# A two-attention transformer block on one core: batch loops written out, score products over all 128 rows, and the mask product in bf16

## The chip, the cores and the metric

The kernel runs on 1 core of one Trainium2 chip. The metric is the device time of one execution in microseconds (us). TensorE's clock has two levels here, 1.2 and 2.4 GHz; a granted clock of 1.00 is the higher one.

## What is computed

Input x is 8 x 512 x 512 in float32. The reference, cut to its steps:

```
attention(x):                        # per batch: seq 512, 16 heads of 32
    Q, K, V = x W^T + (x A^T) B^T    # each with a low-rank term (rank 16) whose matrices an adapter index picks
    Q, K = rope(Q), rope(K)
    P = softmax(where(causal, Q K^T / sqrt(32), -inf))
    return out W_o^T + low-rank term, with out = P V
x1 = layernorm(x + attention(x))
second(x1):                          # hidden 512, feed-forward 2048
    a   = causal attention of rmsnorm(x1) with its own weights, then W_o
    mod = 0.1 tanh(a A)
    h   = rmsnorm(x1)
    return x1 + (silu(h W_in^T + (mod * (h A)) B) * (h W_up^T)) W_down^T
result = layernorm(x1 + second(x1))
```

All products are made in about float32 precision: an operand is split into a high part in float32r (hi) and the rest (lo), and a product is hi*hi + hi*lo + lo*hi.

## The kernel before

The program has three stages one behind the other: `attention_layer` (names `a_`), `gate_layer` (names `b_`, the output projection, first layernorm, second attention down to the modulation) and `mlp_layer` (names `c_`). Each engine runs its own instruction list, and semaphores order them.

Both attention stages have one skeleton. A batch is four groups of four heads. A group is twelve slots, one for each unit; a head has three units, with score widths 512, 384 and 256 + 128 columns (`KEY_MAJOR`, line 36). In slot k of a group the engines do, in this order written out by hand:

- TensorE: `score_t_unit` (line 259), the transposed scores key x q of unit k, and on top of them the causal mask as one more product, eye x colmask, 128 columns wide (line 271). In slots 1 to 7 it also makes `score_unit` (line 174), the plain scores of the next group, which serve only for the row maxima. Then come shares of projections and, two units behind, the product of probabilities and values (`pv_unit`, line 293). In slot 8 it turns the negated row maxima of the next group into rows (`shift_turn`, line 217).
- ScalarE: two exponentials of the scores (lines 281 and 282), copies out of PSUM, and in slot 9 the copy and the transfer of the turned maxima (`shift_copy`, `shift_send`).
- VectorE: the lo part of the probabilities (line 289), and in slots 1 to 7 the masked row maxima (line 199).
- SP: the transfers. `stack_send` (line 242) builds, for two heads at a time and two groups ahead, the operands of the score products.

The stacks are what the change is about. For each head q_stack has q hi in rows 0 to 31, q hi again in 32 to 63 and q lo in 64 to 95; k_stack has key hi, key lo, key hi. One product over these rows makes the three split products at once. Rows 96 to 127 are set once by GpSimd: 0 in q_stack, 1 in k_stack. Rows 112 and 113 of q_stack then take the two parts of the negated row maximum (`shift_send`, line 234), which the ones of k_stack add to the transposed scores. So the plain scores are made over 112 rows (they must not see the maximum), and the transposed ones over 114. A pair of heads is complete when its semaphore `stacked` has risen by 96: six transfers of 16. TensorE waits for that before unit 0 and unit 6 (line 179). ScalarE waits for it before it overwrites the split q or key (lines 745 and 1479).

`batches` (line 65) makes the loop over batches. Batch 0 is written out; then a loop with a branch back runs the same body (batches 1 to 6 in the first stage, 1 to 5 in the second, where `ahead` is 2), and the last one or two are written out again. Inside the loop the batch number is a register, so `apart` (line 54) lets the engine compute the awaited count and then wait for it. With a plain number it is one wait on a constant.

## Time and profile before

| | us |
|---|---|
| median of 3 runs | 2967.54 (2967.21 to 2971.47) |
| the profiled execution | 2964.34 |
| its span, first to last instruction | 2962.5 |
| TensorE busy | 2721.6 (92%) |
| VectorE, ScalarE, GpSimd busy | 1586.3, 1342.3, 645.6 |
| mean granted TensorE clock | 0.955 |

In the rows, PE is TensorE's products, PEld its weight loads, DVE VectorE, ACT ScalarE, POOL GpSimd and SPq the transfers that SP issues. L271 is line 271 of the kernel. A shape like 114x512 is partitions x elements. Products are pipelined, so their durations overlap; the distance between starts tells what one takes from the stream. What stands in brackets behind a row is how long the engine was idle before it and what ended that. "issue" is idle time in which nothing was awaited that the profile shows.

### The profile page before, as it was taken

Reading aid. Unit: us, or ns where it says so; the run is one execution under the profiler, and the core shown is the slowest. Engines: PE = TensorE matmul, PEld = TensorE weight load, DVE = VectorE, ACT = ScalarE, POOL = GpSimd, SP = SyncE. Lnnn points to the kernel's source line nnn. Section 1 sums busy time; section 2 is a strip of 40 time slices with the busy share of each in tenths; the row PEclk is TensorE's granted clock in tenths of the full one; section 3 lists DMA queues with packets and bytes.
Section 4 is the critical chain, followed back from the end, with each engine's and each line's share of the span. In section 5 each row is a group of like instructions: output and inputs, shape, how many; then the busy total and the mean of one; then the engine's idle time right before and its main releaser. Section 6 shows DMA issues by size and latency. Waiting matters only on the chain. (4 is left out here: it accounts for less than half of the span.)

```text
span 2962.5 us, 46172 instructions
## 1 busy us (share of the span) xinstructions
PE 2721.6 (92%) x13840; PEld 2174.2 (73%) x13840; DVE 1586.3 (54%) x4308; ACT 1342.3 (45%) x2755; POOL 645.6 (22%) x528
## 2 busy tenths in 40 slices
PE   5999999999758999999999994999999999999998
PEld 4778777787636777777777762888888888888886
DVE  3777777777634776777777773422222333333333
ACT  2777677766633666656656664311111231111111
POOL 5455555555321122122122112000000000000000
PEclk8999999999867999999999996999999999999999
DMA  5455555555624544544545543311111121111100
GB/s 140 100 135 132 134 116 133 129 129 116 151 83 118 124 96 115 130 90 112 133 91 118 117 89 97 117 58 49 44 44 44 66 87 46 58 44 45 44 29 29
DMA packets 173888, 276.05 MB, mean 93 GB/s; under 512 B 29204, under 2 KB 53524, under 8 KB 173076
## 3 DMA queue, kind: packets, MB, share of 16 engines
q1 hardware_dynamic: 170772, 260.58, 36.3%
q0 software_dynamic: 2304, 12.58, 1.2%
q10 hardware_dynamic: 640, 1.05, 0.1%
q8 instruction: 52, 0.85, 0.1%
q14 instruction: 120, 0.98, 0.1%
HBM read 97.04 MB, written 42.99 MB: 47 GB/s over the span
## 5 line engine op out<-in xcount | busy, mean ns | idle before, releaser
L2224 DVE TENSOR_TENSOR c_product<-c_up_ps,c_gate 128x512 f32<-128x512 f32 x128 | 88.6, 692 | 653.3 <-PE c_up_ps L2290 653.3
L2278 PE MATMUL c_gate_ps<-c_h_split,c_w_split 128*128 128x512 f32 x1536 | 380.8, 397 | 23.6 <-DVE c_w_split L2176 23.6
L2262 PE MATMUL c_down_ps<-c_w_split,c_product_split 128*128 128x512 f32 x1536 | 379.3, 396 | 0.0
L2290 PE MATMUL c_up_ps<-c_h_split,c_w_split 128*128 128x512 f32 x1536 | 378.2, 395 | 0.0
L2278 PEld LDWEIGHTS c_gate_ps<-c_h_split,c_w_split 128*128 128x128 f32 x1536 | 290.0, 189 | 95.3 <-issue 25.3
L2290 PEld LDWEIGHTS c_up_ps<-c_h_split,c_w_split 128*128 128x128 f32 x1536 | 288.4, 188 | 70.0
L2262 PEld LDWEIGHTS c_down_ps<-c_w_split,c_product_split 128*128 128x128 f32 x1536 | 288.9, 188 | 68.6
L281 ACT ACTIVATE b_prob_hi<-b_scores_t_ps 128x384 fp32r<-128x384 f32 (+1 forms) x384 | 201.1, 524 | 266.0 <-PE b_scores_t_ps L271 230.1
L289 DVE TENSOR_TENSOR b_prob_lo<-b_scores_t_ps,b_prob_hi 128x384 fp32r<-128x384 f32 (+1 forms) x384 | 225.8, 593 | 148.9 <-ACT b_scores_t_ps L282 137.3
L289 DVE TENSOR_TENSOR a_prob_lo<-a_scores_t_ps,a_prob_hi 128x384 fp32r<-128x384 f32 (+1 forms) x384 | 226.2, 593 | 145.3 <-ACT a_scores_t_ps L282 140.3
L2148 ACT ACTIVATE c_gate<-c_gate_ps 128x512 f32<-128x512 f32 x128 | 76.4, 597 | 492.4 <-PE c_gate_ps L2285 492.4
L281 ACT ACTIVATE a_prob_hi<-a_scores_t_ps 128x384 fp32r<-128x384 f32 (+1 forms) x384 | 201.3, 524 | 161.7 <-PE a_scores_t_ps L271 136.6
L199 DVE CUSTOM_DVE_ANT_0 b_junk<-b_scores_ps,rowmask 128x512 bf16<-128x512 f32 (+3 forms) x512 | 226.7, 482 | 71.4 <-PE b_scores_ps L185 47.4
L199 DVE CUSTOM_DVE_ANT_0 a_junk<-a_scores_ps,rowmask 128x512 bf16<-128x512 f32 (+3 forms) x512 | 227.0, 484 | 59.4 <-PE a_scores_ps L185 35.8
L2151 ACT ACTIVATE c_product_split<-c_product 128x512 fp32r<-128x512 f32 x128 | 81.0, 633 | 390.5 <-DVE c_product L2224 390.5
L977 PE MATMUL a_lin_ps<-x_split,w_split 128*128 128x512 f32 x768 | 225.7, 412 | 0.4 <-DVE w_split L831 0.4
L268 PE MATMUL b_scores_t_ps<-b_q_stack,b_k_stack 114*128 114x512 f32 (+3 forms) x512 | 159.7, 354 | 51.0 <-DVE b_prob_lo L289 50.0
L1850 PE MATMUL b_lin_ps<-b_h_split,w_split 128*128 128x512 f32 x768 | 203.1, 404 | 1.2 <-ACT b_h_split L1473 1.2
L282 ACT ACTIVATE a_scores_t_ps<-a_scores_t_ps 128x384 f32<-128x384 f32 (+1 forms) x384 | 201.4, 524 | 0.0
L282 ACT ACTIVATE b_scores_t_ps<-b_scores_t_ps 128x384 f32<-128x384 f32 (+1 forms) x384 | 200.7, 523 | 0.0
L268 PE MATMUL a_scores_t_ps<-a_q_stack,a_k_stack 114*128 114x512 f32 (+3 forms) x512 | 154.5, 343 | 42.7 <-DVE a_prob_lo L289 42.6
L268 PEld LDWEIGHTS b_scores_t_ps<-b_q_stack,b_k_stack 114*128 114x128 f32 x512 | 95.9, 200 | 104.4 <-DVE b_prob_lo L289 74.5
(205 smaller groups left out, 4969.8 us busy)
## 6 DMA issues: line engine op xcount, KB each, us to landing
a_q_stack<-a_q_split SPq DMA_DIRECT2D x192, 128.0 KB, 3.2
a_k_stack<-a_k_split SPq DMA_DIRECT2D x192, 128.0 KB, 3.5
b_q_stack<-b_q_split SPq DMA_DIRECT2D x192, 128.0 KB, 3.3
b_k_stack<-b_k_split SPq DMA_DIRECT2D x192, 128.0 KB, 3.6
c_h_stage<-h_t SPq DMA_DIRECT2D x16, 1024.0 KB, 6.2
c_res<-x SPq DMA_DIRECT2D x16, 1024.0 KB, 5.5
c_w_stage<-in_mlp_w POOLq DMA_DIRECT2D x16, 768.0 KB, 4.5
stage<-in_x_t SPq DMA_DIRECT2D x8, 1024.0 KB, 6.4
```

What stands on the lines that cost most here:

```text
L199: last = dve.tensor_tensor_reduce(at.junk[:, k % 2, col:col + width], at.scores_ps[:, k % 2, col:col + width], rowmask[:, SEQ - width:SEQ] ...
L268: pe.matmul(at.scores_t_ps[:, k % 2, col:col + width], key[0:STACK_ROWS, h, kt * P:kt * P + P], q[0:STACK_ROWS, h, kt * P:SEQ], start=(i = ...
L281: act.activation(at.prob_hi[:, k % at.ring, 0:w], at.scores_t_ps[:, k % 2, 0:w], ACT.Exp, scale=SCALE)
L282: act.activation(at.scores_t_ps[:, k % 2, 0:w], at.scores_t_ps[:, k % 2, 0:w], ACT.Exp, scale=SCALE).then_inc(at.exp_done, 1)
L289: dve.tensor_tensor(at.prob_lo[:, k % at.ring, 0:w], at.scores_t_ps[:, k % 2, 0:w], at.prob_hi[:, k % at.ring, 0:w], ALU.subtract).then_in ...
L977: mm = pe.matmul(lin_ps[:, bank, :], w_split[i][:, w, c, g * P:g * P + P], x_split[:, a, c, :], start=(x == 0), stop=False)
L1850: mm = pe.matmul(lin_ps[:, i, :], qk_split[i][:, w, c, g * P:g * P + P], h_split[:, a, c, :], start=(x == 0), stop=(x == 3 * KC - 1))
L2151: act.activation(product_split[:, bank, 0, :], product[:, bank, :], ACT.Copy).then_inc(product_hi, 1)
L2224: dve.tensor_tensor(product[:, bank, :], up_ps[:, bank, :], gate[:, bank, :], ALU.mult).then_inc(product_done, 1)
L2262: mm = pe.matmul(down_ps[:, t, :], product_split[:, kt % 2, a, t * P:t * P + P], w_split[:, w, kt, 2 * KC * P:], start=(kt == 0 and i == 0 ...
L2278: pe.matmul(gate_ps[:, bank, :], w_split[:, w, ft, c * 2 * P:c * 2 * P + P], h_split[run.pair][:, a, c, :], start=(c == 0 and w == 0 and a ...
L2290: mm = pe.matmul(up_ps[:, bank, :], w_split[:, w, ft, c * 2 * P + P:(c + 1) * 2 * P], h_split[run.pair][:, a, c, :], start=(c == 0 and w = ...
```

## The change

- The loop over the batches becomes straight code in both attention stages, and every wait on a computed count becomes a wait on a constant.
- Both kinds of score products take all 128 rows of the stacks. So that the plain scores don't see the row maxima of two groups before, `stack_send` clears rows 112 and 113 of q_stack with one more transfer per pair of heads, from rows 116 and 117, which are always zero. A pair is then complete at 7 x 16 = 112.
- The mask product takes bf16 copies of eye and colmask. eye stays in float32r too, for the turning of the maxima.
- At the start SP waits until GpSimd has also set the q stacks, and TensorE for three constants instead of two.

The diff, without the hunks that only pass `eye_bf` on and with `gate_layer`'s twins of the changed waits left out:

```diff
@@ -38,7 +38,8 @@
 WIDTH = (512, 384, 384)
 
 
-SPLIT_ROWS, SHIFT_ROW, STACK_ROWS = 112, 112, 114
+STACKED = 7 * 16
+SHIFT_ROW, SHIFT_END, SPARE_ROW = 112, 114, 116
 
 
 COS, SIN, EYE, ROWMASK, COLMASK, COUNT = 0, 512, 1024, 1152, 1664, 1792
@@ -64,11 +65,7 @@
 
 def batches(eng, body, ahead=1):
 
-
-    body(0)
-    with eng.Fori(1, BATCH - ahead) as b:
-        body(b)
-    for b in range(BATCH - ahead, BATCH):
+    for b in range(BATCH):
         body(b)
 
 
@@ -97,7 +94,8 @@
         self.x_split = sb("x_split", [P, 2, KC, SEQ], F32R)
         self.rowmask = sb("rowmask", [P, SEQ])
         self.eye = sb("eye", [P, P], F32R)
-        self.colmask = sb("colmask", [P, P], F32R)
+        self.eye_bf = sb("eye_bf", [P, P], BF16)
+        self.colmask = sb("colmask", [P, P], BF16)
         self.lnw = sb("lnw", [P, 2, KC])
 
 
@@ -176,14 +174,14 @@
     h, j = divmod(k, 3)
     n = number(b, g)
     if k % (UNITS // 2) == 0:
-        pe.wait_ge(at.stacked[h // 2], n * 96 + 96)
+        pe.wait_ge(at.stacked[h // 2], n * STACKED + STACKED)
     if k == 0:
         at_least(pe, at.shift_copied, n)
     at_least(pe, at.score_read, n * UNITS + k - 1)
     q, key = at.q_stack[g % 2], at.k_stack[g % 2]
     for i, (qt, col, width) in enumerate(QUERY_MAJOR[j]):
-        mm = pe.matmul(at.scores_ps[:, k % 2, col:col + width], q[0:SPLIT_ROWS, h, qt * P:qt * P + P],
-                       key[0:SPLIT_ROWS, h, 0:(qt + 1) * P], start=(i == 0), stop=True, skip_group_check=True)
+        mm = pe.matmul(at.scores_ps[:, k % 2, col:col + width], q[:, h, qt * P:qt * P + P],
+                       key[:, h, 0:(qt + 1) * P], start=(i == 0), stop=True, skip_group_check=True)
     mm.then_inc(at.score_ready, 1)
 
 
@@ -235,7 +233,7 @@
 
     n = number(b, g)
     act.wait_ge(at.shift_copied, n + 1)
-    act.dma_start(at.q_stack[g % 2][SHIFT_ROW:STACK_ROWS, :, :].bitcast(F32),
+    act.dma_start(at.q_stack[g % 2][SHIFT_ROW:SHIFT_END, :, :].bitcast(F32),
                   at.shift_row[0:2 * GH, :].bitcast(F32)).then_inc(at.shifted, 16)
 
 
@@ -250,13 +248,15 @@
     for r, part in enumerate((0, 0, 1)):
         sp.dma_start(q[32 * r:32 * r + 32, heads, :].bitcast(F32),
                      at.q_split[rows, part, :].bitcast(F32)).then_inc(at.stacked[pair], 16)
+    sp.dma_start(q[SHIFT_ROW:SHIFT_END, heads, :].bitcast(F32),
+                 q[SPARE_ROW:SPARE_ROW + SHIFT_END - SHIFT_ROW, heads, :].bitcast(F32)).then_inc(at.stacked[pair], 16)
     apart(sp, at.ones_set, at.k_ready, n + 1)
     for r, part in enumerate((0, 1, 0)):
         sp.dma_start(key[32 * r:32 * r + 32, heads, :].bitcast(F32),
                      at.k_split[rows, part, :].bitcast(F32)).then_inc(at.stacked[pair], 16)
 
 
-def score_t_unit(pe, at, eye, colmask, b, g, k):
+def score_t_unit(pe, at, eye_bf, colmask, b, g, k):
 
     h, j = divmod(k, 3)
     n = number(b, g)
@@ -265,10 +265,10 @@
     at_least(pe, at.lo_done, n * UNITS + k - 1)
     q, key = at.q_stack[g % 2], at.k_stack[g % 2]
     for i, (kt, col, width) in enumerate(KEY_MAJOR[j]):
-        pe.matmul(at.scores_t_ps[:, k % 2, col:col + width], key[0:STACK_ROWS, h, kt * P:kt * P + P],
-                  q[0:STACK_ROWS, h, kt * P:SEQ], start=(i == 0), stop=False, skip_group_check=True)
+        pe.matmul(at.scores_t_ps[:, k % 2, col:col + width], key[:, h, kt * P:kt * P + P],
+                  q[:, h, kt * P:SEQ], start=(i == 0), stop=False, skip_group_check=True)
     for kt, col, width in KEY_MAJOR[j]:
-        mm = pe.matmul(at.scores_t_ps[:, k % 2, col:col + P], eye[:, :], colmask[:, :],
+        mm = pe.matmul(at.scores_t_ps[:, k % 2, col:col + P], eye_bf[:, :], colmask[:, :],
                        start=False, stop=True, skip_group_check=True)
     mm.then_inc(at.score_t_ready, 1)
 
@@ -596,7 +596,7 @@
             for n, w in ((1, wk_t), (2, wv_t)):
                 for c in range(KC):
                     sp.dma_start(w_stage[n][c], w[:, c, :]).then_inc(w_in[n], 16)
-            sp.wait_ge(rows_zeroed, 2)
+            sp.wait_ge(rows_zeroed, 4)
             send_b(0)
             send_low(0)
             for pair in range(2):
@@ -742,7 +742,7 @@
                 n = number(b, g)
                 act.wait_ge(roped[i], n * 3 + 3)
                 for pair in range(2):
-                    at_least(act, at.stacked[pair], n * 96)
+                    at_least(act, at.stacked[pair], n * STACKED)
                 split = at.k_split if i else at.q_split
                 act.activation(split[:, 0, :], rope_out[i][:, :], ACT.Copy).then_inc(rope_hi[i], 1)
 
@@ -823,6 +823,7 @@
             dve.wait_ge(ids_step, 2 + ADAPTERS)
             dve.tensor_scalar(ids[:, :], count[:, :], 0.0, None, ALU.max).then_inc(ids_step, 1)
             dve.tensor_copy(eye[:, :], square[:, 0, :]).then_inc(const_ready, 1)
+            dve.tensor_copy(eye_bf[:, :], square[:, 0, :]).then_inc(const_ready, 1)
             dve.tensor_copy(colmask[:, :], square[:, 1, :]).then_inc(const_ready, 1)
 
             def weights(n):
@@ -943,7 +944,7 @@
 
         @block.tensor
         def _(pe):
-            pe.wait_ge(const_ready, 2)
+            pe.wait_ge(const_ready, 3)
             pe.wait_ge(rows_zeroed, 4)
             pe.wait_ge(at.ones_set, 3)
 
@@ -1334,7 +1335,7 @@
             sp.dma_start(stage[:, :, :], wo).then_inc(stage_in, 16)
             sp.dma_start(a_full[:, :, :], low_a).then_inc(const_in, 16)
             sp.dma_start(sel[:, :], selector).then_inc(const_in, 16)
-            sp.wait_ge(rows_zeroed, zeroed_before + 2)
+            sp.wait_ge(rows_zeroed, zeroed_before + 4)
             send_b(0)
             send_low(0)
             sp.wait_ge(wo_a_made, 1)
```

## Rows read from the trace of the kernel before

**Rows 1.** Busy time by stretch: us, busy per engine (instructions), clock, DMA share, GB/s.

```profile
0.00:870.00 870.00, 752.29 (x4448) 624.22 (x4448) 584.20 (x1743) 561.34 (x1175) 447.75 (x351) 0.94 0.54 127
870.00:1842.00 972.00, 862.97 (x4656) 658.55 (x4656) 662.25 (x1916) 560.17 (x1191) 190.47 (x164) 0.92 0.48 106
1842.00:2962.00 1120.00, 1106.39 (x4736) 891.41 (x4736) 339.81 (x650) 220.77 (x390) 7.39 (x14) 0.99 0.17 56
```

**Rows 2.** Timeline of TensorE, second stage, line 222: start us, us, instruction.

```profile
1268.56 0.40 PE L222 MATMUL b_scores_ps<-eye,b_shift 128*8 128x128 f32 x4
...
1296.88 0.40 PE L222 MATMUL b_scores_ps<-eye,b_shift 128*8 128x128 f32 x4
...
1607.52 0.40 PE L222 MATMUL b_scores_ps<-eye,b_shift 128*8 128x128 f32 x4
...
1631.67 0.40 PE L222 MATMUL b_scores_ps<-eye,b_shift 128*8 128x128 f32 x4
```

**Rows 3.** Timeline of VectorE at a branch back of the second stage.

```profile
1277.06 0.56 DVE L289 TENSOR_TENSOR b_prob_lo<-b_scores_t_ps,b_prob_hi 128x384 fp32r<-128x384 f32 x1 [2.72 <-issue]
```

**Rows 4.** Busy time and clock right behind that branch, columns as in rows 1.

```profile
1278.00:1284.00 6.00, 6.00 (x23) 4.84 (x23) 4.97 (x16) 4.51 (x11) 0.00 (x0) 0.50 0.93 163
```

**Rows 5.** Timeline of TensorE, first stage, line 222.

```profile
161.26 0.41 PE L222 MATMUL a_scores_ps<-eye,a_shift 128*8 128x128 f32 x4
...
185.95 0.40 PE L222 MATMUL a_scores_ps<-eye,a_shift 128*8 128x128 f32 x4
...
545.21 0.41 PE L222 MATMUL a_scores_ps<-eye,a_shift 128*8 128x128 f32 x4
...
570.99 0.40 PE L222 MATMUL a_scores_ps<-eye,a_shift 128*8 128x128 f32 x4
```

**Rows 6.** Who waited for whom: us in total, times, longest.

```profile
DVE b_junk L199 <- issue: 22.2, 33, 1.3
...
ACT b_prob_hi L281 <- PE b_scores_t_ps L271: 230.1, 216, 3.0
...
ACT b_q_split L1481 <- DMA b_k_stack<-b_k_split: 15.8, 8, 10.2
```

**Rows 7.** Timeline of TensorE, first stage, one single-piece and one two-piece unit.

```profile
406.79 0.34 PE L268 MATMUL a_scores_t_ps<-a_q_stack,a_k_stack 114*128 114x384 f32 x1
406.97 0.22 PE L271 MATMUL a_scores_t_ps<-colmask,eye 128*128 128x128 f32 x1
407.03 1.16 PE L977 MATMUL a_lin_ps<-x_split,w_split 128*128 128x512 f32 x4
...
408.38 0.39 PE L268 MATMUL a_scores_t_ps<-a_q_stack,a_k_stack 114*128 114x256 f32 x2
408.61 0.39 PE L271 MATMUL a_scores_t_ps<-colmask,eye 128*128 128x128 f32 x2
408.83 0.45 PE L977 MATMUL a_lin_ps<-x_split,w_split 128*128 128x512 f32 x1
```

**Rows 8.** Instructions on the tile eye: count, ns min/median/max, first and last start.

```profile
L271 PEld LDWEIGHTS b_scores_t_ps<-colmask,eye x512: 186/191/339, 946.2 to 1803.0; 128*128 128x128 f32 x171
...
L1833 PEld LDWEIGHTS b_lin_ps<-eye,stage x128: 137/144/232, 898.0 to 1678.5; 128*128 128x128 f32 x128
```

**Rows 9.** Timeline of SP's queue, first stage: one pair's q transfers.

```profile
406.22 1.88 SPq L251 DMA_DIRECT2D a_q_stack<-a_q_split  x3
```

**Rows 10.** Timeline of TensorE, first stage: the wait for the key rows.

```profile
413.18 0.49 PE L185 MATMUL a_scores_ps<-a_k_stack,a_q_stack 112*128 112x512 f32 x1 [0.91 <-DMA a_k_stack<-a_k_split]
```

**Rows 11.** Timeline of TensorE: its first product.

```profile
14.03 1.49 PE L961 MATMUL a_lin_ps<-x_split,a_a_split 128*48 128x512 f32 x3 [14.03 <-DVE a_b_split L855]
```

**Rows 12.** Line 623: count, ns min/median/max, first and last start.

```profile
L623 POOL MEMSET a_q_stack<- x2: 1799/1801/1803, 3.5 to 5.3; 32x2048 f32 x2
```

**Rows 13.** Timeline of TensorE, second stage: fp32 transposes between fp32r products.

```profile
1117.07 0.71 PE L1833 MATMUL b_lin_ps<-eye,stage 128*128 128x128 f32 x4
1117.53 0.42 PE L268 MATMUL b_scores_t_ps<-b_q_stack,b_k_stack 114*128 114x384 f32 x1
```

More of the change, by code:

```diff
@@ L428, in attention_layer @@
         ids, w_split, x_stage, x_split = both.ids, both.w_split, both.stage, both.x_split
-        rowmask, eye, colmask = both.rowmask, both.eye, both.colmask
+        rowmask, eye, eye_bf, colmask = both.rowmask, both.eye, both.eye_bf, both.colmask
         a_stage = sb("a_stage", [P, KC, 3 * RANK])
@@ L1020, in step @@
                 for slot in range(UNITS):
-                    score_t_unit(pe, at, eye, colmask, b, g, slot)
+                    score_t_unit(pe, at, eye_bf, colmask, b, g, slot)
                     if not (last and g == GROUPS - 1):
@@ L1146, in gate_layer @@
         values = lin_ps[:, :, :].rearrange("p i (t h d) -> p (i t) h d", t=2, d=RANK)
-        ids, lnw, rowmask, eye, colmask = both.ids, both.lnw, both.rowmask, both.eye, both.colmask
+        ids, lnw, rowmask, eye, eye_bf, colmask = both.ids, both.lnw, both.rowmask, both.eye, both.eye_bf, both.colmask
         wo_split, *qk_split = both.w_split
@@ L1478, in projected @@
                 for pair in range(2):
-                    at_least(act, at.stacked[pair], n * 96)
+                    at_least(act, at.stacked[pair], n * STACKED)
                 split = at.k_split if i else at.q_split
@@ L1889, in step @@
                 for slot in range(UNITS):
-                    score_t_unit(pe, at, eye, colmask, b, g, slot)
+                    score_t_unit(pe, at, eye_bf, colmask, b, g, slot)
                     if slot == 2 and g == 0 and not last:
```

## The prediction, made before the change was run

> **What bounds the kernel now.** I read the stretches first. The span falls into three stages [rows 1]. Up to 870 us runs the first attention, up to 1842 us the second, and the rest is the feed-forward stage, which none of the edited functions reaches: its 1120 us stay. In the two attention stages TensorE is the busiest engine (752 of 870 us and 863 of 972 us), and VectorE and ScalarE have about a third of the time free. So TensorE's stream sets the pace there, broken by places where it waits. Three things are to be priced: what the loops' branches cost, what the mask product costs in that stream, and what the new transfers delay. The sum is made against the profiled execution: 2964.3 us, of which the span is 2962.5. The median of the runs shown is 2967.5, so 3.2 us are added at the end. A change within 0.2% (5.9 us) is about what a measurement of this kernel can't tell from none.
>
> **The loops written out.** A mark that comes once per group is the turning of the shifts (line 222, always in slot 8). The interval from the mark in a batch's last group to the next mark, in the first group of the next batch, holds the batch boundary. In the second stage the loop covers batches 1 to 5, so four boundaries take the branch back. I take one of the middle two as typical: 28.32 us [rows 2]. The boundary from batch 5 to 6 leaves the loop without a branch back and does the same work: 24.15 us [rows 2]. That is 4.2 us for each of four: **16.7 us**. The waits say where it comes from. At that branch VectorE stands 2.72 us on "issue", that is with nothing it waits for in the profile [rows 3], and TensorE, which needs its product, stands too. After that gap TensorE's granted clock is at the lower of its two levels, 1.2 GHz, for 6 us [rows 4]. Part of this is absorbed, which is why I take the interval and not the sum of the pieces. In the first stage the loop covers batches 1 to 6, five branches back. The interval of the middle length is 25.78 us, and the entry from batch 0, without a branch, 24.69 us [rows 5]: 1.09 us, times five, is **5.5 us**. Together 22.2 us.
>
> Inside the loops the waits on a computed count cost VectorE another 22.2 us of "issue" in the second stage, about as much in the first [rows 6]. Written out they become waits on constants. I cost this at nothing: TensorE's own stream hides it. Its bounds are 0 and twice the row, 44 us; I take 0, the end that the busy shares are nearest to, as VectorE is free a third of the time.
>
> **The mask product.** Each of 768 units adds the causal mask with line 271: 1024 products, two in every third unit. In the stream, a product over 384 columns is followed after 0.18 us by the mask product, and that after 0.06 us by the next start [rows 7]. So fp32r already streams 128 columns in 0.06 us, and bf16 can't gain there. In a unit with two pieces the starts stand otherwise: two products take 0.23 us and two masks 0.22 us, so the starts come every 0.11 us [rows 7]. The moving columns of a mask need only 0.06 us of that; what is left is the weights' load, an instruction of its own that can't run further ahead than the product before. If bf16 makes this load shorter than 0.06 us, each of the two masks starts 0.05 us sooner: 0.10 us per such unit. The product behind the last mask loads fp32r weights and still comes 0.11 us after it, so single masks bring nothing. 256 units times 0.10 us are 25.6 us, the upper end. The lower end is nothing, if the load takes as long as now; a loss is a rival below. How much of it reaches the end? In the second stage ScalarE's exponentials waited for the mask product in 216 of 384 units [rows 6]; there the gain is passed on in full, elsewhere only through TensorE's stream. Between half and all I take 0.7: 25.6 x 0.7 = **17.9 us**. I take the fast load because the nearest row for another kind of operand, the plain fp32 transposes, shows that the load depends on the kind: 144 ns against 191 ns for this one [rows 8]. No row has a bf16 load.
>
> The Trainium skill has two sentences on this that disagree for this kernel, both in "TensorE: Matmul & The Clock Gate". Its section "LDWEIGHTS (loading the stationary operand)" counts columns alone, which is 107 ns for 128 columns of any type; by it the mask gains nothing and rival (1) comes true. Its section "Weight-path perf modes — Fast Weight Load (FWL) and DoubleRow" says that the load goes about twice as fast when there are 128 weights and the type is not FP32; by it a load would take an estimated 53 ns and the whole term is there. No run here shows a bf16 load yet.
>
> **128 rows.** The score products now use all 128 rows instead of 112 and 114. Rows seem to have no price: two-piece units load 114 rows and 128 rows at the same 0.11 us [rows 7]. Cost: none. Bounds: nothing below, and above half a nanosecond for each of 14 to 16 rows in 2048 products, 16 us, were rows paid like columns (0.18 us for 384); I take none, as the loads show.
>
> **The clearing transfers.** They are two more on SP's queue in each of 64 groups, between the three for q and the three for key, each 0.6 us of issue, as three take 1.88 us [rows 9]. Everything behind them on that queue moves: the key rows, the store of the group before, the next gather. Mostly this is hidden, because the stacks are sent a group before they are used; without that cover 128 x 0.6 = 77 us. The cover is gone once per batch of the first stage: behind the low-rank sends the key rows come late, and TensorE waits 0.91 us for them [rows 10]. 0.6 us more in each of seven batches: 4.2 us. A longer wait also makes a low clock behind it likelier; two more drops of some 3 us at half speed [rows 4] cost 3 us. In the second stage ScalarE waits for the stacks before it splits the next q, 8 times [rows 6]. Its wait grows by the second pair's 0.6 us; half of 8 x 0.6 reaches the end, with the first pair's in part behind SP's own waits: 2 us. Together **9.2 us** lost. Bounds: 2, since SP's register work for waits goes away, and 15, if the clock drops in every batch. The wait for four zeroed tiles instead of two and the second constant copy lie at the start, where TensorE's first product waits 14.03 us for VectorE's split of the adapters [rows 11]; without that cover they cost the two memsets, 3.6 us [rows 12].
>
> **Sum.** 2964.3 - 22.2 - 17.9 + 9.2 = 2933.4 us, plus 3.2: **2937 us**.
>
> **The rivals.**
> (1) *The bf16 load is no faster.* For it: no row shows one, and loads of 114 and 128 rows take the same time, so columns seem to rule. Against it: rows 8. The mask term is gone: 2964.3 - 22.2 + 9.2 + 3.2 = **2954 us**.
> (2) *The change of kind stalls the array.* Where a bf16 product stands between fp32r ones, TensorE would have to run empty before it and behind it. The price is the part of a 128-column product that now overlaps the next: 0.22 us long, 0.06 us to the next start, so 0.16 us, twice in 768 units: 246 us, and the time would be **3200 us**. It decides from 13 us / 768 = 17 ns a unit. Against it: four fp32 transposes pass between fp32r products, and the fp32r product starts 0.46 us after their first, 0.115 us each, without a gap [rows 13].
> (3) *Straight code stalls too.* The instructions of written-out batches come from memory just the same, and stands like the 2.72 us could come at other places as often as now. Then the 22.2 us are not gained: 2964.3 - 17.9 + 9.2 + 3.2 = **2959 us**, or 2977 us with a slow load. Against it: batch 6 of the second stage is written out today, and its boundary has none of it [rows 2].
>
> **How the numbers follow.** Forecast 0.58, with 2922 to 2945 as its own range; (1) 0.30, (3) 0.07, (2) 0.05. The whole range takes in the forecast with the whole mask gain and a small loss (2964.3 - 22.2 - 25.6 + 4 + 3.2 = 2924), a few us below it for the register waits that I cost at nothing, and rival (1) with the transfers' upper bound (2954 + 6 = 2960): 2918 to 2960. Faster by more than 0.2% (below 2961.6): both main cases and the smaller part of (3), 0.90. Within 0.2%: 0.03. Slower: (2) and the rest of (3), 0.07.
>
> **What would show it.** The intervals of line 222 across every batch boundary should be near 24.2 us in the second and 24.7 us in the first stage, and VectorE's "issue" stands of 2.7 us gone. The mask's load should be well under 190 ns, and two-piece units should take 0.35 us to the next start instead of 0.45. The wait for the key rows in the first stage should be longer by up to 0.6 us. The forecast is wrong if mask loads stay at 190 ns, if gaps stand around line 271, if "issue" shows up elsewhere, or if the key rows' wait is followed by low clock in most batches.

## The result, and the profile after

The changed kernel took 2932.7 us (median; 2929.3 to 2934.3), the kernel before 2967.4 us beside it. The ratio is 0.9879, with a 95% interval of 0.9862 to 0.9896: 1.2% faster, and 34.6 us by the medians. The forecast was 2937 us, with 2918 to 2960 as its range.

| | before | after |
|---|---|---|
| median, us | 2967.4 | 2932.7 |
| the profiled execution / its span | 2964.3 / 2962.5 | 2934.3 / 2932.4 |
| TensorE products busy / weight loads busy | 2721.6 / 2174.2 | 2685.4 / 2053.0 |
| VectorE, ScalarE busy | 1586.3, 1342.3 | 1584.6, 1335.6 |
| instructions in the trace | 46172 | 41577 |
| mean granted TensorE clock | 0.955 | 0.969 |

Here are the profile after's stretches, with the columns of [rows 1]. The first three are the stages, and the fourth is where the branch's low clock stood before [rows 4].

```profile
0.00:860.00 860.00, 747.85 (x4448) 572.05 (x4448) 584.90 (x1744) 557.63 (x1173) 441.30 (x348) 0.95 0.53 127
860.00:1812.00 952.00, 830.83 (x4656) 590.79 (x4656) 660.49 (x1917) 557.66 (x1194) 196.38 (x167) 0.96 0.47 111
1812.00:2932.00 1120.00, 1106.77 (x4736) 890.16 (x4736) 339.22 (x649) 220.34 (x389) 7.39 (x14) 0.99 0.17 56
...
1276.00:1284.00 8.00, 8.00 (x49) 5.95 (x47) 5.90 (x16) 5.91 (x13) 2.60 (x2) 1.00 0.93 228
```

The feed-forward stage is what it was, 1120 us. The second attention stage gives 20 us (972 to 952) and the first 10 (870 to 860). Counted more closely, from each attention's first mark (the turning of the shifts, line 222 before) to its last, the second goes from 847.6 to 825.3 us, the first from 759.6 to 755.9, and the way from one to the other from 114.3 to 110.3. So almost all of the gain lies in the second stage and ahead of it, and the first stage gives 4 us.

The changed kernel's timeline, all engines. Line 220 is now the mark (222 before), 268 the transposed scores, 271 the mask (PEld its loads), 978 the first projections; SPq lines 249, 251 and 255 are q's transfers, the clearing and key's transfers.

```profile
406.61 0.34 PE L268 MATMUL a_scores_t_ps<-a_q_stack,a_k_stack 128*128 128x384 f32 x1
406.79 0.23 PE L271 MATMUL a_scores_t_ps<-colmask,eye_bf 128*128 128x128 bf16 x1
406.83 1.18 PE L978 MATMUL a_lin_ps<-x_split,w_split 128*128 128x512 f32 x4
...
408.20 0.39 PE L268 MATMUL a_scores_t_ps<-a_q_stack,a_k_stack 128*128 128x256 f32 x2
408.43 0.28 PE L271 MATMUL a_scores_t_ps<-colmask,eye_bf 128*128 128x128 bf16 x2
408.43 0.12 PEld L271 LDWEIGHTS a_scores_t_ps<-colmask,eye_bf 128*128 128x128 bf16 x2
408.52 1.18 PE L978 MATMUL a_lin_ps<-x_split,w_split 128*128 128x512 f32 x4
409.54 0.39 PE L985 MATMUL a_lin_ps<-a_low_stack,a_b_stack 128*128 128x512 f32 x1
...
405.87 1.88 SPq L249 DMA_DIRECT2D a_q_stack<-a_q_split  x3
407.79 0.66 SPq L251 DMA_DIRECT2D a_q_stack<-a_q_stack  x1
408.49 1.85 SPq L255 DMA_DIRECT2D a_k_stack<-a_k_split  x3
...
371.27 0.59 ACT L315 ACTIVATE a_pv_raw<-a_pv_ps 65x512 f32<-65x512 f32 x1 [2.78 <-DMA a_sums<-a_pv_raw]
...
544.21 0.40 PE L220 MATMUL a_scores_ps<-eye,a_shift 128*8 128x128 f32 x4
...
570.58 0.40 PE L220 MATMUL a_scores_ps<-eye,a_shift 128*8 128x128 f32 x4
...
1254.80 0.40 PE L220 MATMUL b_scores_ps<-eye,b_shift 128*8 128x128 f32 x4
...
1277.89 0.55 DVE L289 TENSOR_TENSOR b_prob_lo<-b_scores_t_ps,b_prob_hi 128x384 fp32r<-128x384 f32 x1
...
1278.60 0.41 PE L220 MATMUL b_scores_ps<-eye,b_shift 128*8 128x128 f32 x4
...
1577.95 0.40 PE L220 MATMUL b_scores_ps<-eye,b_shift 128*8 128x128 f32 x4
...
1601.76 0.41 PE L220 MATMUL b_scores_ps<-eye,b_shift 128*8 128x128 f32 x4
```

Four things are to be read there. *The boundaries*: from 1254.80 to 1278.60 is 23.80 us, where the branch had made it 28.32 [rows 2]; the last, from 1577.95 to 1601.76, is 23.81 (24.15 before). VectorE's L289 at 1277.89 has no bracket: the stand of 2.72 us [rows 3] is gone, and the granted clock behind it is full instead of half. *The first stage's boundaries* moved little: 544.21 to 570.58 is 26.37 us, 25.78 before [rows 5]; the five at issue have a mean of 25.5, before 25.7. *The mask*: in the two-piece unit the next product comes 0.09 us after the two masks began, where it was 0.22 [rows 7]. That next product itself then takes a little longer: from its line's first start to the next line's is 1.02 us (408.52 to 409.54) instead of 0.98. The net in this unit is 0.09 us. *ScalarE at 371.27* stands 2.78 us for the transfers of the group's sums. Before, it reached this place later and stood 0.45 us. The two rows of the kernel before on which the last two readings rest (its timeline):

```profile
409.81 0.39 PE L984 MATMUL a_lin_ps<-a_low_stack,a_b_stack 128*128 128x512 f32 x1
...
371.20 0.59 ACT L315 ACTIVATE a_pv_raw<-a_pv_ps 65x512 f32<-65x512 f32 x1 [0.45 <-DMA a_sums<-a_pv_raw]
```

The changed kernel's instructions on the identity in bf16 (count, ns min/median/max, first and last start):

```profile
L271 PEld LDWEIGHTS a_scores_t_ps<-colmask,eye_bf x512: 95/96/149, 74.0 to 840.5; 128*128 128x128 bf16 x171
...
L271 PEld LDWEIGHTS b_scores_t_ps<-colmask,eye_bf x512: 95/96/147, 939.8 to 1772.0; 128*128 128x128 bf16 x171
```

The bf16 load is 96 ns, half of 191 [rows 8]. The changed kernel's waits (us in total, times, longest):

```profile
ACT b_prob_hi L281 <- PE b_scores_t_ps L271: 205.1, 181, 3.0
...
PEld a_scores_t_ps L271 <- issue: 42.3, 195, 0.5
...
ACT a_pv_raw L315 <- DMA a_sums<-a_pv_raw: 27.8, 21, 3.2
...
ACT b_q_split L1482 <- DMA b_k_stack<-b_k_split: 20.8, 8, 10.4
...
ACT b_pv_raw L315 <- DMA b_sums<-b_pv_raw: 17.6, 8, 4.0
...
PE a_scores_ps L183 <- DMA a_k_stack<-a_k_split: 15.5, 11, 7.6
```

VectorE's wait on "issue" in the score maxima (22.2 us in 33 pieces, [rows 6]) is gone. The 42.3 us of "issue" ahead of the mask's loads are new, but they are idle time of the loads alone: TensorE's products have no stand on "issue" in either attention. In the second stage ScalarE waits less for the mask product: 181 times for 205 us, before 216 times for 230. It waits more for the sums' transfers: 27.8 and 17.6 us, where the kernel before had these two rows (its waits):

```profile
ACT a_pv_raw L315 <- DMA a_sums<-a_pv_raw: 10.1, 10, 1.9
...
ACT b_pv_raw L315 <- DMA b_sums<-b_pv_raw: 7.8, 4, 3.0
```

And the wait for the key rows, which the prediction expected to grow, is 15.5 us in total in the first stage, as before (15.9), though in 11 pieces instead of 9.

### The profile page after: what moved, and what is told of

It reads as the page before. It is cut to its first block and busy times, and to the rows that moved or that the text cites. A ratio compares the mean times of both kernels' runs of the same rounds, so it can differ in the third digit from the quotient of the medians.

```text
span 2932.4 us, 41577 instructions
## 1 busy us (share of the span) xinstructions
PE 2685.4 (92%) x13840; PEld 2053.0 (70%) x13840; DVE 1584.6 (54%) x4309; ACT 1335.6 (46%) x2755; POOL 645.1 (22%) x528
## 5 line engine op out<-in xcount | busy, mean ns | idle before, releaser
L289 DVE TENSOR_TENSOR a_prob_lo<-a_scores_t_ps,a_prob_hi 128x384 fp32r<-128x384 f32 (+1 forms) x384 | 226.3, 594 | 151.6 <-ACT a_scores_t_ps L282 149.4
L289 DVE TENSOR_TENSOR b_prob_lo<-b_scores_t_ps,b_prob_hi 128x384 fp32r<-128x384 f32 (+1 forms) x384 | 226.1, 594 | 135.8 <-ACT b_scores_t_ps L282 134.3
L268 PE MATMUL b_scores_t_ps<-b_q_stack,b_k_stack 128*128 128x512 f32 (+3 forms) x512 | 153.3, 340 | 50.0 <-DVE b_prob_lo L289 45.6
L268 PE MATMUL a_scores_t_ps<-a_q_stack,a_k_stack 128*128 128x512 f32 (+3 forms) x512 | 152.8, 340 | 42.3 <-DVE a_prob_lo L289 42.1
L183 PE MATMUL a_scores_ps<-a_k_stack,a_q_stack 128*128 128x512 f32 (+3 forms) x512 | 147.7, 371 | 20.2 <-DMA a_k_stack<-a_k_split 15.5
```

What stands on the lines that cost most here:

```text
L183: mm = pe.matmul(at.scores_ps[:, k % 2, col:col + width], q[:, h, qt * P:qt * P + P], key[:, h, 0:(qt + 1) * P], start=(i == 0), stop=True ...
L268: pe.matmul(at.scores_t_ps[:, k % 2, col:col + width], key[:, h, kt * P:kt * P + P], q[:, h, kt * P:SEQ], start=(i == 0), stop=False, skip ...
L289: dve.tensor_tensor(at.prob_lo[:, k % at.ring, 0:w], at.scores_t_ps[:, k % 2, 0:w], at.prob_hi[:, k % at.ring, 0:w], ALU.subtract).then_in ...
```

## The experiments

Twelve runs, in three groups; "before" was run beside each group (medians 2966.3, 2965.7 and 2964.3 us), and the ratios are to it. They are built from three parts: the loops, the bf16 mask, and the 128 rows with their clearing. None changes what is computed. The last column is the mean granted clock over all executions of a kernel; that of the kernel before was 0.959 beside each group.

| kernel | loops | mask | clearing | rows | median, us | ratio to before | clock |
|---|---|---|---|---|---|---|---|
| e1_unroll | written out | fp32r | none | 112, 114 | 2939.2 | 0.9911 [0.9895, 0.9927] | 0.963 |
| e2_mask | as before | bf16 | none | 112, 114 | 2956.0 | 0.9965 [0.9951, 0.9979] | 0.959 |
| e3_rows | as before | fp32r | yes | 128, 128 | 2969.1 | 1.0012 [1.0003, 1.0021] | 0.964 |
| e4_unroll_mask | written out | bf16 | none | 112, 114 | 2932.8 | 0.9876 [0.9857, 0.9895] | 0.963 |
| e5_no_bf16 | written out | fp32r | yes | 128, 128 | 2936.9 | 0.9903 [0.9883, 0.9922] | 0.967 |
| e6_two_per_turn | two batches a turn | fp32r | none | 112, 114 | 2963.1 | 0.9987 [0.9976, 0.9998] | 0.962 |
| e7_three_clears | written out | bf16 | three a pair | 128, 128 | 3027.6 | 1.0201 [1.0183, 1.0219] | 0.958 |
| e8_one_mask | written out | bf16, one product | none | 112, 114 | 2925.8 | 0.9861 [0.9843, 0.9878] | 0.963 |
| e9_clears_only | written out | bf16 | yes | 112, 114 | 2938.4 | 0.9910 [0.9894, 0.9926] | 0.963 |
| e10_t_rows | written out | bf16 | none | 112, 128 | 2924.5 | 0.9862 [0.9844, 0.9880] | 0.969 |
| e11_one_mask_t_rows | written out | bf16, one product | none | 112, 128 | 2916.7 | 0.9840 [0.9823, 0.9857] | 0.968 |
| e12_changed | written out | bf16 | yes | 128, 128 | 2932.1 | 0.9888 [0.9871, 0.9905] | 0.967 |

The rows are those of the plain and of the transposed score products.

### One part at a time

**e1_unroll**: the kernel before with its loops written out.

```diff
-    body(0)
-    with eng.Fori(1, BATCH - ahead) as b:
-        body(b)
-    for b in range(BATCH - ahead, BATCH):
+    for b in range(BATCH):
         body(b)
```

> The kernel before with only the batch loops written out; 112 and 114 rows, no clearing transfers, fp32r mask. Terms as predicted: 22 us less than before, about 2945 us; the batch boundaries of the second stage fall from 28.3 to 24.2 us between marks, those of the first from 25.8 to 24.7 us. Rival A (the loops are the whole change and the mask product's gain is hidden): about 2933 us. Rival B (the stands at the branches only move, since other waits end as late): 2960 us or more.

Measured: 0.9911, 26 us less, the largest of the three parts. The second stage's boundaries are 24.0 to 24.3 us where they were 24.2 to 28.4 (all but the last, 22.8 us, which had no branch before either), the first stage's 24.2 to 25.3. The seven boundaries of the second stage together give 16.4 us (183.7 to 167.3), while the rest of that stage takes as long as before (663.8 and 665.0 us), with all the waits on computed counts gone. So there it is the branch that costs. In the first stage the boundaries give 5.0 us (177.3 to 172.3) and the rest 2.9 us (582.2 to 579.3).

**e2_mask**: the kernel before with the mask product in bf16.

```diff
-        self.colmask = sb("colmask", [P, P], F32R)
+        self.eye_bf = sb("eye_bf", [P, P], BF16)
+        self.colmask = sb("colmask", [P, P], BF16)
...
-        mm = pe.matmul(at.scores_t_ps[:, k % 2, col:col + P], eye[:, :], colmask[:, :],
+        mm = pe.matmul(at.scores_t_ps[:, k % 2, col:col + P], eye_bf[:, :], colmask[:, :],
```

> The kernel before with only the mask product in bf16; loops, 112 and 114 rows. Terms as predicted: 18 us less than before, about 2949 us, low clock at every branch of the second stage as before. Rival A (mask gain hidden behind the exponentials and VectorE): 2963 us or more. Rival C (the shorter TensorE stretches give more than their own length, because waits behind them shrink too and the clock stays up): 2940 us or less.

Measured: 0.9965, 10 us less. The gain is real and is a little over half of the 18 us forecast.

**e3_rows**: the kernel before with the score products over 128 rows and the clearing transfers.

```diff
+    sp.dma_start(q[SHIFT_ROW:SHIFT_END, heads, :].bitcast(F32),
+                 q[SPARE_ROW:SPARE_ROW + SHIFT_END - SHIFT_ROW, heads, :].bitcast(F32)).then_inc(at.stacked[pair], 16)
...
-        mm = pe.matmul(at.scores_ps[:, k % 2, col:col + width], q[0:SPLIT_ROWS, h, qt * P:qt * P + P],
-                       key[0:SPLIT_ROWS, h, 0:(qt + 1) * P], start=(i == 0), stop=True, skip_group_check=True)
+        mm = pe.matmul(at.scores_ps[:, k % 2, col:col + width], q[:, h, qt * P:qt * P + P],
+                       key[:, h, 0:(qt + 1) * P], start=(i == 0), stop=True, skip_group_check=True)
```

> The kernel before with only the score products over 128 rows and the clearing transfers; loops, fp32r mask. Terms as predicted: 9 us more than before, about 2976 us, most of it at the waits for the key rows. Rival A (hidden): within 3 us of before. Rival D (the later gathers hold ScalarE's copy of the first head's sums, which the prediction had costed at nothing): 15 us or more above before, with several us of idle time before line 315 released by the sums' transfer in each batch.

Measured: 1.0012, 3.6 us slower by the ratio (2.8 by the medians); 1.0000 lies just outside the interval. The expected 9 us didn't come. ScalarE's wait for the first stage's sums, rival D's sign, did: 25.4 us in total, where the kernel before has 10.1. The small sum is made of two terms with opposite signs, as e9 and e10 show.

**e4_unroll_mask**: the changed kernel without its third part, that is, loops and mask together.

> The changed kernel without its rows and clearing transfers: loops written out, bf16 mask, 112 and 114 rows. Terms as predicted: 9 us less than the changed kernel, about 2924 us. Rival A: the same as the changed kernel, 2931 to 2935 us. Rival D: 15 us or more below the changed kernel, 2918 us or less.

Measured: 0.9876, 2932.8 us, which is rival A's number and 9 us above the expected 2924. The product of e1 and e2 is 0.9911 x 0.9965 = 0.9876: the two parts add up. The changed kernel's 0.9879 lies inside its interval: the third part bought nothing that can be measured.

### Which part of the mask, of the loop, of the transfers

**e5_no_bf16**: the changed kernel with the mask product in fp32r again (the two lines of e2 the other way round).

> The changed kernel with the mask product back in fp32r; loops written out, 128 rows and clearing transfers stay. So far the mask alone brought 10 us in the loops (0.9965) and the same beside written-out loops (0.9911 against 0.9876). If its gain is worth the same beside the transfers, this kernel takes 10 us more than the changed one, 2941 to 2945 us. If the transfers eat the room that the mask makes (rival), it takes less than 5 us more, below 2938 us.

Measured: 0.9903, against 0.9879 and 0.9888 (e12) for the changed kernel: bf16 is worth 4 to 7 us in company. The median of 2936.9 us lies in the rival's range (below 2938) and short of the 10 us expected. The intervals overlap, so only e2 shows the mask's gain by itself in the time.

**e6_two_per_turn**: the kernel before, with two batches in each turn of the loop. It halves the branches and leaves the waits on computed counts within a turn.

```diff
-    with eng.Fori(1, BATCH - ahead) as b:
-        body(b)
-    for b in range(BATCH - ahead, BATCH):
+    pairs = (BATCH - 1 - ahead) // 2
+    with eng.Fori(0, pairs) as i:
+        body(i * 2 + 1)
+        body(i * 2 + 2)
+    for b in range(1 + 2 * pairs, BATCH):
         body(b)
```

> The kernel before with two batches in each turn of the loop: the branches back fall from 5 to 2 in the first stage and from 4 to 1 in the second, while the waits on computed counts stay in all but at most one batch of a stage. If the branches are what costs (my theory): 3 x 1.1 + 3 x 4.1 = 15.6 us of the 26 us of all loops written out, about 2950 us. If the waits on computed counts are (rival): 4 us or less, 2962 us or more.

Measured: 0.9987, 2.7 us less by the medians: a miss for the 2950 us of my theory, and the rival's number. Its boundaries tell why it is still not the rival's mechanism. In the second stage one branch back is left, with 27.90 us; the two boundaries inside a turn take 24.13 and 24.11, the two written out 24.04 and 24.02. So the computed waits cost these boundaries nothing, as costed, and the whole price there is the branch's. But in the first stage the two branches that are left now have boundaries of 29.17 and 28.79 us, where five of 25.1 to 26.0 stood. The timeline of e6_two_per_turn at one branch of each stage:

```profile
360.96 0.56 DVE L291 TENSOR_TENSOR a_prob_lo<-a_scores_t_ps,a_prob_hi 128x384 fp32r<-128x384 f32 x1 [4.07 <-issue]
361.25 0.79 PE L270 MATMUL a_scores_t_ps<-a_q_stack,a_k_stack 114*128 114x512 f32 x1 [2.82 <-issue]
...
1279.72 0.79 PE L270 MATMUL b_scores_t_ps<-b_q_stack,b_k_stack 114*128 114x512 f32 x1 [2.31 <-issue]
...
1280.34 0.56 DVE L291 TENSOR_TENSOR b_prob_lo<-b_scores_t_ps,b_prob_hi 128x384 fp32r<-128x384 f32 x1 [3.04 <-issue]
```

VectorE stands 4.07 us on "issue" in the first stage, and TensorE has "issue" stands of its own, of 2.82 and 2.31 us; in the kernel before it had stood 2.58 us at the second stage's branch, waiting for VectorE's L289. In the first stage the branches over a body twice as long cost more, 3.6 us each instead of about 1.1, and from mark to mark it got 7.4 us longer (759.6 to 767.0). In the second stage the one branch left costs 3.8 us (27.90 less 24.1), no more than one of the four before (about 4.1). Its seven boundaries together gave 12.8 us, but the stage got only 7.8 us shorter (847.6 to 839.7): its other groups took 5.0 us more (663.8 to 668.8), for which the trace shows no single cause. So the number of branches alone is not the measure. Why the first stage's cost more is not shown; no run varied the body's length by itself.

The Trainium skill's page "Runtime: NRT & Kernel Launch", section "Instruction fetch mechanics", says that instructions are fetched ahead in sequence at little cost, and that a taken branch whose target isn't in the engine's current window of two blocks stalls it until the target has come. The traces agree in both halves: stands of 2.72 and 4.07 us at branches, and in the changed kernel no stand of VectorE where they were. That a fetch is what VectorE stands for, no row shows.

**e7_three_clears**: the changed kernel with three clearing transfers a pair instead of one; the other two write zeros over rows that are zero.

```diff
-STACKED = 7 * 16
+STACKED = 9 * 16
...
-    sp.dma_start(q[SHIFT_ROW:SHIFT_END, heads, :].bitcast(F32),
-                 q[SPARE_ROW:SPARE_ROW + SHIFT_END - SHIFT_ROW, heads, :].bitcast(F32)).then_inc(at.stacked[pair], 16)
+    for row in (SHIFT_ROW, SPARE_ROW + 2, SPARE_ROW + 4):
+        sp.dma_start(q[row:row + SHIFT_END - SHIFT_ROW, heads, :].bitcast(F32),
+                     q[SPARE_ROW:SPARE_ROW + SHIFT_END - SHIFT_ROW, heads, :].bitcast(F32)).then_inc(at.stacked[pair], 16)
```

> The changed kernel with three small transfers per pair of heads where it has one; the two others write zero rows over zero rows. The prediction had one cost 9 us. Alone in the looped kernel rows and transfers cost 3.5 us. If the price grows in proportion: 7 to 18 us more than the changed kernel. If there is a threshold (SP's queue is behind the need by then, so each further 0.6 us counts in full in the first stage, 2 x 0.6 x 2 in each of 28 groups): 30 us or more. If the transfers are hidden (rival): within 4 us.

Measured: 1.0201, 95 us above the changed kernel (3027.6 against 2932.7), which is the expected threshold case. The waits of e7_three_clears:

```profile
ACT a_pv_raw L316 <- DMA a_sums<-a_pv_raw: 53.1, 25, 5.3
...
PE a_scores_ps L183 <- DMA a_k_stack<-a_k_split: 35.7, 24, 7.6
ACT b_pv_raw L316 <- DMA b_sums<-b_pv_raw: 34.8, 9, 5.2
```

256 more transfers at 0.66 us each are 169 us of SP's queue, and 95 us of that come through to the end. The first stage takes most of it, 818.7 us from mark to mark against 755.9; the second takes 853.5 against 825.3. Both consumers of what this queue sends wait longer: TensorE for the key rows 24 times instead of 11, ScalarE for the sums 53 us instead of 28. The price of a transfer on this queue is far from linear: 95 us for 256 of them, against 10 us for the first 128 (e9).

**e8_one_mask**: e4 with the two masks of a two-piece unit made by one bf16 product over 256 columns (one load).

```diff
-        self.colmask = sb("colmask", [P, P], BF16)
+        self.colmask = sb("colmask", [P, 2, P], BF16)
...
-    for kt, col, width in KEY_MAJOR[j]:
-        mm = pe.matmul(at.scores_t_ps[:, k % 2, col:col + P], eye_bf[:, :], colmask[:, :],
-                       start=False, stop=True, skip_group_check=True)
+    pieces = len(KEY_MAJOR[j])
+    to = at.scores_t_ps[:, k % 2, :].rearrange("p (i n) -> p i n", i=2)[:, 0:pieces, 0:P]
+    mm = pe.matmul(to, eye_bf[:, :], colmask[:, 0:pieces, :], start=False, stop=True, skip_group_check=True)
```

> Written-out loops, 112 and 114 rows, no clearing transfers, and the mask of a two-piece unit as one bf16 product of 256 columns, so with one load of eye in place of two. In the stream the bf16 mask pieces came 0.05 us apart and no load shorter than a piece can make them come faster, so TensorE's stream gains at most 0.01 us a unit and the time should be within 4 us of the kernel with written-out loops and bf16 mask (2933 us). Rival: each load or instruction of its own costs 0.03 to 0.05 us in two-piece units; then 5 to 12 us less, 2921 to 2928 us.

Measured: 0.9861 against e4's 0.9876, 2925.8 us: 7 us less by the medians and 4 by the ratios, with intervals that overlap. The median is in the rival's range, and the trace says why the expectation missed. It had the two bf16 masks 0.05 us apart; the trace of the changed kernel has them 0.07 us apart (median of 257 pairs, 67 ns; 111 ns before). In the timeline of e8_one_mask the next product now starts 0.04 us behind the mask's start, where it was 0.09:

```profile
406.11 0.28 PE L270 MATMUL a_scores_t_ps<-colmask,eye_bf 128*128 128x256 bf16 x1
406.15 0.48 PE L977 MATMUL a_lin_ps<-x_split,w_split 128*128 128x512 f32 x1
```

### The third part taken apart

**e9_clears_only**: e4 with the clearing transfers, the rows as before.

```diff
-STACKED = 6 * 16
+STACKED = 7 * 16
...
+    sp.dma_start(q[SHIFT_ROW:SHIFT_END, heads, :].bitcast(F32),
+                 q[SPARE_ROW:SPARE_ROW + SHIFT_END - SHIFT_ROW, heads, :].bitcast(F32)).then_inc(at.stacked[pair], 16)
```

> Written-out loops and bf16 mask with the clearing transfers but without the 128 rows (plain scores over 112 rows, transposed over 114). The first stage should carry the transfers' price: between the first and last mark of line 222's kind about 756 us, as in the changed kernel, against 746 us without them. If the transfers are all there is to the price, and the 128 rows gave back what the changed kernel has gained elsewhere, this kernel takes 2940 us or more. If rows do nothing and the second stage's low clock is chance (rival): as the changed kernel, 2931 to 2935 us.

**e10_t_rows**: e4 with the transposed scores over 128 rows, and no clearing.

```diff
-        pe.matmul(at.scores_t_ps[:, k % 2, col:col + width], key[0:SHIFT_END, h, kt * P:kt * P + P],
-                  q[0:SHIFT_END, h, kt * P:SEQ], start=(i == 0), stop=False, skip_group_check=True)
+        pe.matmul(at.scores_t_ps[:, k % 2, col:col + width], key[:, h, kt * P:kt * P + P],
+                  q[:, h, kt * P:SEQ], start=(i == 0), stop=False, skip_group_check=True)
```

> Written-out loops and bf16 mask, no clearing transfers, plain scores over 112 rows, but the transposed scores over all 128 (rows 114 to 127 of q_stack are zero, so nothing need be cleared). If rows keep the clock up (in three pairs of profiles the second stage was less at low clock with 128 rows: 31 against 61, 3 against 20, 14 against 31 us): 3 to 8 us less than without the rows, 2925 to 2930 us, and under 20 us of low clock in the second stage. If rows do nothing (rival): 2930 to 2935 us.

**e11_one_mask_t_rows**: e8 with the same edit as e10. **e12_changed**: the changed kernel once more, beside them.

> The kernel with one mask product per unit and the transposed scores over all 128 rows. If rows keep the clock up: 2919 to 2923 us, the fastest of all. If rows do nothing: 2923 to 2929 us, as with 114 rows.

> The changed kernel again, beside the three others on one chip. Theory: 2930 to 2935 us, and from the first to the last mark 753 to 758 us in the first stage. If the second stage's 14 us of low clock were chance, this profile shows another figure there, 5 to 35 us.

Measured: e9 0.9910 against e4's 0.9876, so the clearing costs 10 us (2938.4 us, nearer to the theory's 2940 than to the rival); e10 0.9862, so the rows save 4 (2924.5 us, the theory's case). e12 came as expected. Both attentions from the first mark to the last, columns as in [rows 1]: first e4_unroll_mask,

```profile
61.50:807.56 746.06, 693.58 (x4265) 540.61 (x4265) 540.03 (x1645) 521.29 (x1102) 398.77 (x310) 0.98 0.57 130
922.07:1754.87 832.80, 778.53 (x4357) 556.30 (x4357) 620.72 (x1802) 520.72 (x1110) 166.36 (x138) 0.97 0.50 110
```

then e9_clears_only,

```profile
59.91:815.75 755.84, 700.20 (x4265) 542.14 (x4266) 541.29 (x1645) 521.10 (x1101) 398.37 (x310) 0.98 0.55 129
927.97:1759.81 831.84, 778.36 (x4357) 556.88 (x4357) 620.07 (x1802) 520.30 (x1110) 166.40 (x138) 0.97 0.48 111
```

and e10_t_rows.

```profile
61.73:809.73 748.00, 694.02 (x4266) 539.00 (x4266) 540.80 (x1645) 521.16 (x1102) 399.08 (x310) 0.98 0.57 130
922.76:1745.98 823.22, 766.86 (x4356) 546.53 (x4357) 615.86 (x1802) 519.78 (x1110) 168.18 (x139) 0.99 0.50 111
```

The clearing costs 9.8 us in the first stage (746.06 to 755.84) and nothing in the second. The rows do nearly the reverse: 1.9 us more in the first stage, 9.6 us less in the second, at a clock of 0.99 instead of 0.97 with the same number of products. The rows' gain is not in TensorE's waits, which the stretch less the busy time gives as 54.3 and 56.4 us, but in its busy time, 778.53 to 766.86. In the waits of e4 ScalarE stands 18.3 us for the first stage's sums, in e9 22.3. For the second stage's it is 13.5 and 17.6 us, the same growth, and there it costs nothing. About half of the 9.8 us lies in the seven batch boundaries (4.4 us), and the rest is spread over the other groups.

e11 took 2916.7 us, a ratio of 0.9840 [0.9823, 0.9857]. It is the fastest of all, below both ranges expected; its median is 47.6 us below before's and 15.4 us below that of e12. Its interval doesn't meet that of the changed kernel beside it (0.9871 to 0.9905), so it beats both kernels.

## Why the prediction was right, and where it was not

By the steps of the prediction:

- **Loops, -22.2 us: right, a little low.** 26 us alone (e1). The intervals fell to 23.8 us in the second stage, with no stand of VectorE and no low clock behind it, which was the reasoning. The reasoning left out that ScalarE stood too: in the kernel before it has four stands on "issue" of 2.5 to 2.8 us at the same four branches (10.3 us in all, line 281), and these are gone as well. The second stage's 16.7 us measured 15.3 (847.6 to 832.3 in e1), the first's 5.5 measured 8.0, and 2.4 more came in the way between the two.
- **Waits on a computed count, nothing: right in the second stage.** The 22.2 us of "issue" are gone, e6's boundaries with and without them take the same 24.1 us, and e1's groups outside the boundaries got no shorter there. In the first stage those groups gave 2.9 us, and no run tells whether these waits had a part in it.
- **The mask, -17.9 us: right mechanism, mis-sized.** The load is 96 ns instead of 191. The prediction asked for one shorter than 0.06 us, which it is not; yet two masks in a row start 0.07 us apart instead of 0.11, for two loads overlap (two take 0.12 us in the row above). The unit shown gains 0.09 us where 0.10 was worked out, and 256 x 0.09 would be 23 us of TensorE's stream. Over both attentions less came free. From e1 to e4, at nearly the same clock, TensorE's busy time fell from 703.4 + 781.8 us to 693.6 + 778.5, by 13 us. From e5 to the changed kernel it fell by 14 us (1479.7 to 1466.1), from before to e2 by 14 (1494.8 to 1480.4). So the factor that failed is the first one, the 25.6 us taken from a single unit; of the 14 us free in e2, 10 reached the end, which is the share of 0.7. In company less may reach it (e5). The rows of e1_unroll, columns as in [rows 1], to be set against e4's above:

```profile
62.50:814.12 751.62, 703.37 (x4266) 588.62 (x4266) 541.09 (x1645) 522.84 (x1101) 399.63 (x310) 0.97 0.56 129
925.97:1758.25 832.28, 781.83 (x4356) 594.12 (x4357) 617.56 (x1802) 521.11 (x1110) 166.55 (x138) 0.98 0.50 110
```

- **128 rows, no cost: mis-sized, with a gain that the bounds excluded.** "Nothing below" was wrong: from e9 to e12 the ratio fell by 0.0022, from e4 to e10 by 0.0014 and from e8 to e11 by 0.0021, 4 to 7 us each. The intervals of each pair overlap; that all three have the sign is what the reading rests on, with the stretches above and the clocks (below). The products themselves cost the same: over 384 columns the next start came after 0.18 us with 114 rows and with 128.
- **The clearing transfers, +9.2 us: right size, but not by its own terms.** e9 shows 10 us, all in the first stage; the 2 us for the second didn't come. The key rows' wait, for which I had priced 4.2 us, grew by 1.2 us from e4 to e9 (16.0 to 17.2). ScalarE's wait for the sums of the group before grew by 4.0 us. The prediction had named the gather's move on SP's queue and costed it at nothing. But the same growth in the second stage cost nothing, and of the 9.8 us only 3.1 are in TensorE's waits; the other 6.6 are in its busy time (693.58 to 700.20), at the same clock. So what carries the price is not shown, and that the total came out at 9.2 is luck.
- **Start-up, nothing: right.** The first mark came at 61.9 us, before at 61.5.

The sum held (2937 against 2932.7) partly by luck, because errors cancelled: the mask gave 8 us less than costed, the loops 4 more and the rows about 6 more.

In the first stage ScalarE has a longer wait, which may have taken back part of the gain. At 371 us ScalarE came to its copy of the sums 2.3 us earlier than before (2.78 us of waiting instead of 0.45) and waited for a transfer that landed when it had before, at 371.2 us. Across the runs this wait is 10.1 us in total in the kernel before, 15.1 in e1, 18.3 in e4, 22.3 in e9, 25.4 in e3 and 27.8 in the changed kernel: some of it comes from the engines being faster, some from the clearing ahead of the gather on SP's queue. That both feed it is read from these totals; no run took the wait itself away. It would fit the first stage's boundaries, which moved by only 0.2 us on average in the changed kernel.

**The rivals.** (1), a load no faster, is refuted by the 96 ns. The Trainium skill's two sentences on it, which the prediction set against each other ("TensorE: Matmul & The Clock Gate"), come out so: with the section "Weight-path perf modes — Fast Weight Load (FWL) and DoubleRow", which says about twice as fast, the trace agrees in the ratio (191 to 96 ns); with the section "LDWEIGHTS (loading the stationary operand)", which counts columns alone and gives 107 ns for 128, it agrees for neither kind, and the measured 191 and 96 ns decide. The prediction's estimate of 53 ns from the two together was too short as well. (2), the array stalled by a change of kind, is refuted: the mask starts 0.18 us behind the fp32r product, the same as before, and the next 0.04 us behind it. (3), straight code that stalls, is refuted: in both attentions of the changed kernel VectorE has no stand on "issue" at all. ScalarE has seven of 1.5 us in the second stage, ahead of its copy of the turned maxima (line 228), where the kernel before shows two (2.1 us in all). They are not new time: its idle time ahead of that copy, whatever ended it, is 40.8 us there, before 42.3. The 13 us from which the prediction has (2) decide is worked out there from nothing.

**What the 128 rows do, and what stays open.** The clock can be read from every execution and not only from the profiled ones. With 128 rows the mean granted clock is higher in each of five pairs: e4 to e10 (0.963 to 0.969; single executions 0.959 to 0.967 and 0.965 to 0.971), e8 to e11 (0.963 to 0.968; 0.963 to 0.964 and 0.965 to 0.970), e9 to e12 (0.963 to 0.967), e1 to e5 (0.963 to 0.967, with clearing) and before to e3 (0.959 to 0.964, with clearing). In the first two only the transposed products differ, so these alone do it; the plain ones alone were not tried. From this the gain can be estimated: 0.963 is 7.4% of the time at the lower of two levels, 0.967 is 6.6%. That is 23 us less of it, worth at most half, 12 us, where 4 to 7 us were measured.

That the clock is what makes these kernels faster is the best supported reading and not shown. In the single profiles, the second stage's time at half speed (from its second mark to the first of its last four) goes with its length for e4 and e9 (31 and 34 us, length 832 to 833), e10 and e12 (7 us, 822 to 823). But e8, with 112 and 114 rows, has 17 us and a length of 823.0, and e11, the fastest, 24 us and 820.2. Why more rows go with a higher clock no run shows.

## What to carry to other kernels

Price a loop by its branch, measured as the interval across one boundary with the branch against one without, and write it out where the engine that stands is one that TensorE waits for; fewer and longer turns were no substitute here (2.7 us of 26). Make the operand whose load sets the pace a 16-bit one where its values are exact in it, and better, make one product of two. Before a transfer is put on a full queue, list everything behind it, the next gather included, and look for the consumer that already waits there: here the third part of the change took back what it gave. The better kernel, e11, leaves the clearing out, keeps the transposed scores over 128 rows and makes one mask product of two.

## What the runs showed of the hardware that I had not expected

- Over a body of two batches VectorE's longest stand at a branch back was 4.07 us, over one batch 2.82. One branch of the first stage cost 1.1 us before and 3.6 in e6 (28.98, the mean of its two boundaries with a branch, less 25.41, the mean of its five others, is 3.57). In the second stage it was 4.1 us and 3.8.
- Two more small transfers a pair (e7) cost 95 us, the first one 10. With 0.66 us for each issue, more than half of the added 169 us reaches the end.
- A bf16 load takes 96 ns and an fp32r load 191, and products that follow one another on such loads start 0.07 and 0.11 us apart.
- With more rows in its products a kernel had a higher granted clock in all five pairs of runs (0.959 or 0.963 to 0.964 to 0.969), though a product's distance to the next is the same at full clock. Why is open, as said above.
